# A graph-attention layer and a mixture of eight experts on one core: the gated rows are formed ahead of the fourth low half, and the bias operands grow from 48 (40 used) to 128 rows

## The reference, cut to what matters

```python
x = x + gnn(layernorm(x), ...)          # 384 tokens of 1024, 16 heads, masked attention
x = x + ffn(layernorm(x)[None], ...)[0]

def _expert(x, g, b, W1, b1, W2, b2, Wo, bo):
    x = _layernorm(x, g, b)
    x1 = x @ W1 + b1
    x2 = jnp.clip(x @ W2 + b2, -20.0, 20.0)
    hidden = jnp.clip(x1 * (x2 * jax.nn.sigmoid(x2)), -10000.0, 10000.0)
    return jnp.clip(hidden @ Wo + bo, -10000.0, 10000.0)
```

## Time and profile before

| | |
|---|---|
| median of 3 runs | 569.07 us (567.72 to 569.13) |
| the profiled execution, its own time | 569.24 us |
| its span, first to last instruction | 567.5 us |
| busy: TensorE, VectorE, ScalarE, GpSimd | 513.8, 407.6, 282.3, 149.1 us |
| moved by DMA | 106.32 MB, mean 187 GB/s |

### The profile page before, as it was taken

How to read it: one execution, slowest core, us unless ns; L and a number is a source line. 1 busy time by engine, 2 the same in 40 slices (tenths; PEclk the granted TensorE clock), 3 DMA queues, 4 the chain that set the end, 5 groups by cost and what they waited for, 6 DMA issues and landing times.

```text
span 567.5 us, 6818 instructions
## 1 busy us (share of the span) xinstructions
PE 513.8 (91%) x2579; PEld 445.8 (79%) x2579; DVE 407.6 (72%) x675; ACT 282.3 (50%) x407; POOL 149.1 (26%) x129
## 2 busy tenths in 40 slices
PE   3899999999999998989998979449999999999994
PEld 3899889999999998878787868437776776776773
DVE  6658877744334435789997867775987987987995
ACT  2435223423323443677776104335787687687540
POOL 5100333542334330122223922222012022000362
PEclk9899999999999999689999989658999999999988
DMA  8278663333443343010006521495859889879452
GB/s 308 107 267 361 230 234 136 118 130 126 150 149 105 118 151 114 1 74 2 0 1 209 179 62 69 137 343 205 319 220 397 318 328 390 330 288 374 149 185 112
DMA packets 20929, 106.32 MB, mean 187 GB/s; under 512 B 4720, under 2 KB 5104, under 8 KB 11168
## 3 DMA queue, kind: packets, MB, share of 16 engines
q1 hardware_dynamic: 15328, 91.53, 42.6%
q0 software_dynamic: 3696, 7.96, 4.3%
q10 hardware_dynamic: 1872, 6.39, 3.1%
HBM read 98.96 MB, written 6.91 MB: 187 GB/s over the span
## 4 chain that ended last, share of the span: by engine, by line
PE 60%; DVE 19%; ACT 8%; issue 6%; POOL 4%; DMA 1%; ACTq 0%; DVEq 0%; POOLq 0%
PE ps L1098 53%; DVE lo L712 10%; PE ps L1161 3%; ACT xg L629 3%; POOL xres L471 2%; ACT hi L545 2%; PE ps L1201 2%; DVE hh L1022 1%; ACT xg_hi L633 1%; DMA xg<-z_rows,slot_tok 1%; DVE small L717 1%; ACT sg L638 1%; DMA xin<-in_x 1%; DVE x2c L1011 1%; DVE ht_lo L977 1%
## 5 line engine op out<-in xcount | busy, mean ns | idle before, releaser
L712 DVE TENSOR_TENSOR lo<-raw,hi 128x2048 fp32r<-128x2048 f32 x70 | 159.2, 2289 | 60.6 <-ACT hi L545 60.5
L545 ACT ACTIVATE hi<-raw 128x2048 fp32r<-128x2048 f32 x70 | 131.7, 1913 | 76.0 <-PE ps L1098 65.1
L438 POOL DMA_INDIRECT mask_rows<-colf,bits x48 | 56.2, 1171 | 134.7 <-DMA mask_rows<-colf,bits 83.0
L1098 PE MATMUL ps<-xt_hi,hi 128*128 128x384 f32 x192 | 65.2, 339 | 2.3 <-DVE xt_lo L728 2.3
L1098 PE MATMUL ps<-xt_hi,lo 128*128 128x384 f32 x192 | 65.2, 340 | 0.0
L1098 PE MATMUL ps<-xt_lo,hi 128*128 128x384 f32 x192 | 65.2, 340 | 0.0
L1098 PE MATMUL ps<-hi,xg_hi 128*128 128x512 f32 x128 | 53.1, 415 | 1.5 <-DVE xg_lo L972 1.5
L1098 PE MATMUL ps<-lo,xg_hi 128*128 128x512 f32 x128 | 51.3, 401 | 0.0
L1098 PE MATMUL ps<-hi,xg_lo 128*128 128x512 f32 x128 | 51.2, 400 | 0.0
L1098 PE MATMUL ps<-t_hi,lo 128*128 128x384 f32 x128 | 43.0, 336 | 0.0
L1098 PE MATMUL ps<-t_lo,hi 128*128 128x384 f32 x128 | 43.0, 336 | 0.0
(11 more groups left out here) (207 smaller groups left out, 1065.8 us busy)
## 6 DMA issues: line engine op xcount, KB each, us to landing
raw<-in_wf SPq DMA_DIRECT2D x42, 1024.0 KB, 7.2
raw<-in_wg SPq DMA_DIRECT2D x28, 1024.0 KB, 5.4
xfb<-in_wf SPq DMA_DIRECT2D x6, 1024.0 KB, 7.3
src_i<-in_srcb ACTq DMA_DIRECT2D x4, 768.0 KB, 4.9
dst_i<-in_dstb ACTq DMA_DIRECT2D x4, 768.0 KB, 9.9
y_rows<-y SPq DMA_DIRECT2D x6, 512.0 KB, 3.0
xin<-in_x SPq DMA_DIRECT2D x3, 512.0 KB, 4.6
xres<-in_x SPq DMA_DIRECT2D x3, 512.0 KB, 4.8
```

What stands on the lines that cost most here:

```text
L438: pool.indirect_dma_start(out=mbuf[:, :], out_offset=bass.IndirectOffsetOnAxis(ap=bits[:, 1, g:g + 1], axis=0), in_=colf[:, 5, g:g + 1], i ...
L545: act.activation(hi[SLOT[c]][:, :], raws[RAW[c]], ACT.Copy).then_inc(hi_done, 1)
L712: dve.tensor_tensor(lo[SLOT[c]][:, :], raws[RAW[c]], f32(hi[SLOT[c]][:, :]), ALU.subtract).then_inc(lo_done, 1)
L1098: ins = pe.matmul(o, a[s], b[m], start=first and n == 0, stop=last and n == 2)
```

## The change

Two things are changed. On VectorE the split of nxt[3], if there is one, now stands behind the product and clip of the gated rows `hh`, where it joins the splits of nxt[4] and nxt[5]; before it stood in front of them. And the operands of the bias matmuls have 128 rows in place of 40: `brow_f`, `brow`, `sels` and `selx` are allocated with 128 rows, and all matmuls, copies and clears take all of them. Rows that hold no bias are zero. The parts inside `crowded` (L1064 to L1090, L1327) run only where an expert has over 128 tokens.

```diff
-                brow_f = sb(rowbuild, "brow_f", [48, 2 * D], F32)
+                brow_f = sb(rowbuild, "brow_f", [P, 2 * D], F32)
...
-            brow = sb(ffn, "brow", [48, 2 * D], F32R)
+            brow = sb(ffn, "brow", [P, 2 * D], F32R)
...
-            sels = sb(ffn, "sels", [48, NE], F32)
-            selx = sb(ffn, "selx", [48, 3, P], F32R)
+            sels = sb(ffn, "sels", [P, NE], F32)
+            selx = sb(ffn, "selx", [P, 3, P], F32R)
...
-                pool.tensor_copy(selx[:, slot, :], sels[:, e:e + 1].to_broadcast([48, P])).then_inc(sel_set, 1)
+                pool.tensor_copy(selx[:, slot, :], sels[:, e:e + 1].to_broadcast([P, P])).then_inc(sel_set, 1)
...
                 if e + 1 < NE:
                     tokens_lo(e + 1, (e + 1) % 2)
-                if nxt[3]:
-                    split_lo(nxt[3])
                 dve.wait_ge(silu_done, e + 1)
                 dve.wait_ge(chunk_used, up_chunks(e) + 4)
                 if e:
                     dve.wait_ge(h_turned, e)
                 link(dve.tensor_tensor(hh[:, :], B[0], sg[:, :], ALU.mult))
                 dve.tensor_scalar(hh[:, :], hh[:, :], 10000.0, -10000.0, ALU.min, ALU.max).then_inc(h_ready, 1)
-                for k in nxt[4:6]:
+                for k in nxt[3:6]:
                     if k:
                         split_lo(k)
...
-                pe.matmul(bank, selx[0:40, e % 3, :], brow[0:40, cols], start=True, stop=False)
+                pe.matmul(bank, selx[:, e % 3, :], brow[:, cols], start=True, stop=False)
...
-                    pe.matmul(B[3 + part], selx[0:40, e % 3, :], brow[0:40, cols], start=True, stop=False)
+                    pe.matmul(B[3 + part], selx[:, e % 3, :], brow[:, cols], start=True, stop=False)
```

More of the change, by code:

```diff
@@ L1064, in _ @@
                 dve.tensor_copy(fr[:, :, 7:8], over_gate[:, :, bass.ds(e, 1)])
-                dve.tensor_copy(selx[:, 0, :], sels[:, bass.ds(e, 1)].to_broadcast([48, P])).then_inc(over_sel, 1)
+                dve.tensor_copy(selx[:, 0, :], sels[:, bass.ds(e, 1)].to_broadcast([P, P])).then_inc(over_sel, 1)
                 dve.wait_ge(over_sel, e + 1)
@@ L1325, in over_sum @@
             def over_sum(bank, act_hi, act_lo, tiles, chunk0, bias_cols):
-                pe.matmul(bank, selx[0:40, 0, :], brow[0:40, bias_cols], start=True, stop=False)
+                pe.matmul(bank, selx[:, 0, :], brow[:, bias_cols], start=True, stop=False)
                 for k in range(tiles):
```

## The result

The changed kernel took 561.82 us in the median of 4 runs (559.77 to 562.32), the kernel before 569.09 (567.72 to 569.13): ratio 0.9863, 95% interval 0.9843 to 0.9883. Predicted were 561.8 us and a range of 559.7 to 564.6. All medians are of all executions, while the ratios leave out two slow ones of the kernel with the wider operands alone, of 586.30 and 1253.18 us.

A forecast was written before the change was run, and what follows sets the result against it. Bound: a circle between VectorE and ScalarE in each expert, no engine full. 6.4 + 0.3 + 0.35 + 0.1 + 0.1 = 7.25, say 7.3 us off 569.24 gives 561.9; median 561.8 us, range 559.7 to 564.6.

The forecast's parts named there:

- Expert 7 and the hidden rows: Late in the expert stage: expert 7's 0.31 us wait filled, 0.3 us, and a closing hidden-row wait, 0.1 us.
- the group in expert 0: Bias matmuls ahead of the product that `hh` waits for in expert 0: wider operands save 0.35 us.
- the last pair: Two bias matmuls of `down(7)`, started after expert 6's output clip: wider operands save 0.1 us.
- the circle: VectorE and ScalarE waiting on each other from `x2c` to `x2c`: 21.14 us an expert, 20.07 after the change.
- The reordering: `hh` fills VectorE's wait ahead of nxt[3] in experts 1 to 6: 6 x 1.07 = 6.4 us saved.
- The wider operands: Bias groups save 0.35 us each, so TensorE needs 19.1 us an expert, not 20.14, and stays under 20.07.
- Height is free: Clearing `brow_f` with more rows goes by columns and costs 0 to +0.1 us.
- (a): Rival: wider operands save nothing, TensorE becomes the bound, only its waits for `hh` go, 5.05 us: 564.0 us; chance 0.14.
- Its threshold: Rival (a) decides if a bias group saves under 0.13 us; 22 groups would have to give about 2.9 us.
- (b): Rival: DMA becomes the bound, needing 370 GB/s at share 0.93; about 568.5 us; chance 0.07, in full or in part.
- (c): Rival: the moved wait brings TensorE to half clock for over 20 us, slower, about 574 us; chance 0.05.
- (d): Half-clock stretch in `down(7)` falls elsewhere: 1.6 us less (560.2) or more (563.4); chance 0.70 together with the forecast.

The follow-up runs named there:

- the earlier clip: Clip of x @ W2 moved ahead of the split of nxt[1], against the changed kernel: 554.17 us, ratio 0.9757 to the kernel before; again 555.95 us, 0.9751.

## Why the prediction was right, point by point

**Budget.** I use the second profile of the changed kernel (span 559.9), whose clock, like before's, is low in the last `down`. Against 567.5 the parts are: up to `hh` of expert 0 0.71 us less (396.83, 396.12); from there to `x2c` of expert 1 nothing (10.47 both); from it to `x2c` of expert 7 6.41 (128.11, 121.70); from there to the output clip of expert 6 0.55 (9.42, 8.87); from that to the last clip 0.20 (9.50, 9.30); the end 0.27 more (13.17, 13.44). The sum is 7.60. A part of the 0.71 isn't the change: over the twelve profiles `hh` of expert 0 starts between 395.02 and 398.36 us, as the clock falls in the stages ahead.

**That it came within 0.02 us is luck.** The terms were not known that well. Expert 7 and the hidden rows gave 0.15 more than I took, the group in expert 0 0.05 more and the last pair perhaps 0.1, while the end took back 0.27 that I had left out; and the executions of the changed kernel alone spread over 2.5 us. What holds is the mechanism and the 6.4 of the circle.

**The reordering**, 6 x 1.07 = 6.4: measured 6.41, by the mechanism named. Expert 7 and the hidden-row wait, 0.3 + 0.1: measured 0.55.

**The wider operands** as a condition, not as a gain: right, and this is what the prediction stood on. But the steady period gives only 0.10 us an expert of it (20.15 with the reordering alone, 20.05 with both); 1.24 of the 1.69 us in the stretch lie in the last expert, which the prediction didn't say. I took 0.35 us for a group, and it is 0.40. The excess that I had read off was not all of it, and not all of that went. In `up`, from the first of eight transposes to the bias matmul it was 0.97 us and is 0.79; to the next matmul 0.42 and now 0.31, to the one after 0.34 and now 0.24. So 0.18 us ahead of the bias matmul had been left out, and 0.08 behind it stays, where I had named 0.23 us as the sign. In `down` the excess of 0.09 + 0.20 + 0.10 is all gone. TensorE's own need is 18.9 us an expert, not 19.1. The term is mis-sized by some 15% and changes little, since it lies off the circle.

**Expert 0 and the last pair**, 0.35 and 0.1: of the 0.71 ahead of `hh` of expert 0 the group is 0.40 (from `x2c` to `hh` 7.16 us before, 6.76 in this profile) and the rest isn't the change; the last pair gave at most 0.2.

**Height is free** for the clear of `brow_f`: 1.811 us with 128 rows, 1.804 with 48.

**Rivals.** (a), that the wider operands save nothing, is refuted, and its price was right: the reordering alone took 564.2 where (a) said 564.0, and in the stretch it gave 5.27 us where (a) said 5.05. Its threshold was not: 6.4 + 0.3 + 0.1 - 5.05 = 1.75 us over 22 groups is 0.08 us a group, not 0.13, and the profiles with the reordering alone and with both parts differ by 1.69 there. The rule behind it, of TensorE: Matmul & The Clock Gate in the Trainium skill, Part 3, The mechanism, is that a weight load overlaps running matmuls only where row groups differ. It doesn't hold here: 128-row bias matmuls have 0.23 us to their neighbours in `down`. (b), DMA, is refuted at 390 GB/s. (c), a long stretch at half clock, didn't come; short ones came in the kernel with waits of some 2 us. (d) came as a spread inside the changed kernel: the profiled execution of 559.77 had the last `down` at full clock, its second profile at half.

**What I had left out** is the end of the kernel. I took it to keep its length. In the first profile it grew from 13.17 to 14.3 us, because VectorE's last low halves fell under GpSimd's sums and took 4.00 us in place of 2.59; with the clock of the second profile the growth is 0.27. So the gain of 1.6 us from the clock in `down(7)` (7.74 us from the output clip of expert 6 to the last clip, 9.30 in the second profile) was partly paid back there.

## What to carry to other kernels

Where no engine is full, look for the circle through their lists, and fill the wait on it with work whose inputs are ready; moving the work from one such wait to another gives nothing. Before you count such a gain, add up what the next engine needs without its own wait: here it was 20.14 against 20.07 us, and two changes worth 4.4 and nothing alone gave 7.3 together. Add it up for the last round too, where an engine that ran without slack is what the end waits for. Where matmuls of few rows stand between full ones, try them padded with zeros to 96 or 128 rows, and look again for the next order then: the clip one place earlier gave 6 to 7 us more, and with 40 rows nothing.

## What the runs showed of the hardware that was not expected

- A bias matmul of few rows between matmuls of 128 rows has one of two prices: 64 rows are as 40 (0.43, 0.34 us to the next two), 96 rows as 128 (0.31, 0.24).
- VectorE's `scalar_tensor_tensor` on 128x1024 took 1.28 us alone and 3.31 to 3.51 us when it began during one of GpSimd's `tensor_tensor` sums or together with it. It ended 1.1 us after the sum did. One that began first (537.73, GpSimd's sum at 537.98, second profile of the earlier clip) took its 1.28 us.
- With waits of some 2 us in most experts TensorE fell to its lower level for stretches between 400 and 530 us (means of 0.91 and 0.83); with waits of 1.0 us, or none, it didn't in any profile here. In `down(7)` it fell in eight of the twelve profiles.
- A DMA share of 0.97 to 0.99 at 384 to 390 GB/s held nothing up, with seven buffers for the loads (the earlier clip).
